# Two PSUM banks in turn for G and V, two long scans, and a state sum made in PSUM

## The chip, the cores and the metric

The kernel runs on one core of one Trainium2 chip. The metric is the device time of one execution in microseconds (us); lower is better. Each engine (PE is TensorE, DVE is VectorE, ACT is ScalarE, POOL is GpSimd) works through its own instruction list in order, and the lists are tied by semaphores alone.

## The reference: what is computed

One sequence of 2048 tokens of width 128 goes through two residual layers. The first is a damped-oscillator state space layer with 4 heads, head width 64 and state size 128; the second is a dense mixture of 8 experts plus a shared one.

```
# layer 1, on layernorm(x); for each head, p = 64 channels, n = 128 states
v = (v - dt*A*y + dt*u*Bv) / denom          # denom = 1 + dt*kdamp + dt^2*A, per head, token and n
y = y + dt*v + dt*u*By
o = sum_n y*Cy + sum_n v*Cv                 # By, Bv and Cy, Cv are l2-normalised over 256
out = (o + skip*u) * silu(z) @ W_out.T
# layer 2, on layernorm(x): softmax router, top 2 of 8 experts (gelu MLPs), plus the shared expert
```

## The kernel before, in words

**Tiling.** Tokens are cut into 16 tiles of 128, and four tiles make a group, so there are four groups g. A (tile, head) pair is a q; a group has 16 of them. The recurrence inside a tile is written with products of 2x2 transition matrices, which are formed for the 16 q of a group at once, forwards and backwards from the middle of a tile (`MID` = 64).

**Stages.** Before group 0 there is a prologue, which prepares the coefficients of that group. Each group then has three stages. The *step loop* runs 32 matrix steps on DVE (L1008), between which DVE also adds the experts of the group before (L1230). The *mid stage* is a software pipeline over k = 0 to 23 (`MID_STEPS`): at k below 16 it handles q = 16g + k, and `due(g, k, lag)` says which tile's work with a given lag falls on k; it puts tile c at k = 3 + 4c + lag. The coefficients of the next group (the "front", `front_early`) are made at fixed k inside it. The *expert stage* follows: second layernorm, router and expert matmuls on PE, gelu on ACT, with the next group's matrices and step loop on DVE at the same time.

**One q in the mid stage.** PE projects B and C into one of two PSUM banks (`proj`, L513) as soon as DVE's `products` of two q earlier have freed it. ACT squares the bank (`pair`, L767). DVE scales half of it in place (`pair`, L1105) and multiplies it with the transition products (`products`, L1122 and L1124). POOL adds these to W and V (`wv`, L1376 and L1379). PE then makes G = V'W in bank GG (L536) and transposes V into bank VT (L540), both in `gv`. DVE masks G (`causal_g`, L1112) and ACT copies V' out (`vt_copy`, L773). `gv(q)` waits for the mask of q-1 and, for its transposes, for the copy of q-1, since there is one bank GG and one bank VT.

**The order on each engine** is the order in which the code calls these, per k: PE: `op`, `proj(k+1)`, `norms_back`, `norms_C`, `tail`, `norms`, `tail_T`, `gv(k-1)`, front. ACT: `pair(k)`, small copies, front, then `vt_copy(k-1)`, with the copy of the norm sums behind each fourth one. DVE: `state_sum`, `pair(k)`, `residual`, `tile_out`, `causal_g(k-2)`, `products(k)`, `state`, `add_skip`, front. POOL: `ubar`, `gates`, `crossings`, `wv(k)`.

**A tile's state.** `tail` makes the tile's contribution in bank RR with ub (64 columns of a head) stationary and the V' of two halves, 256 columns, moving (L572). ACT copies RR to `rts` (L802), `tail_T` transposes it back in four pieces into RR (L598), and DVE's `state_sum` adds it to the state `xi` into `zz` (L1132). `state` applies the tile's transition to `zz` (L1142 to L1146). The output part of `tail` goes to bank OO (L587, L589) and needs `xi`.

**The coefficients.** The log denominators of a group lie in `lden` in 16 segments of 129. DVE makes the running sum of each with one scan (L969, sixteen in all, over k = 15 and 16), one subtraction of the middle column follows (L977, k = 17), ACT takes two exponentials (L717, L720), and DVE makes beta and alpha from them (L983, L991).

Of the kernel before, what the change touches and what calls it, by code (L numbers as in the profile page):

```python
# [32 lines left out]
ALU = mybir.AluOpType  # L33
# [36 lines left out]
PRODUCTS, NORMS, NORMS_C, TAIL, TAIL_T, OUT = 1, 2, 4, 4, 6, 7  # L70
MASK, UBAR, GATES, TILE_OUT, STATE_SUM, STATE = 2, 3, 5, 6, 7, 3
# [25 lines left out]
def build(nc, x, w_inT, dw_wT, dw_bT, w_outT, skipT_in, dt_bias, theta_rawT, k_rawT,  # L97
          router_w, router_b, sw1, sb1T, sw2, sb2, rw1, rb1T, rw2, rb2, out):
    ctx = ExitStack()
    with ctx:  # L100
# [26 lines left out]
        ones = sb("ones", 128, 1)  # L127
        eps_l2 = sb("eps_l2", 128, 1)
# [8 lines left out]
        lraw = sb("lraw", 128, KP)  # L137
        lx = sb("lx", 128, KP)
        le = sb("le", 128, KP)
        lp = [sb(f"lp{i}", 128, KP) for i in range(2)]  # L140
        dtts = [sb(f"dtt{i}", 128, KP) for i in range(2)]
        dtr = sb("dtr", KP, TS)
        lden = sb("lden", NS, PC)
        de = sb("de", NS, 2 * PC)
        ab = sb("ab", NS, 2 * PC)
        DTN, LCS = 1, PC
# [8 lines left out]
        tf = [sb(f"tf{i}", 128, GT * NE * NE) for i in range(2)]  # L155

# [18 lines left out]
        rts = sb("rts", 128, 2, 2, NS)  # L175
# [24 lines left out]
        w9T = sb("w9T", NX, GC)  # L200
# [3 lines left out]
        def bank(name):  # L204
# [3 lines left out]
        GG = bank("GG")  # L208
        VT = bank("VT")
# [21 lines left out]
        scan_done, inv_den, beta_done = sem("scan_done"), sem("inv_den"), sem("beta_done")  # L231
# [4 lines left out]
        gv_done, gm_done, vt_done, norm_done, row_done, ub_done, gate_done = (sem(s) for s in  # L236
            ("gv_done", "gm_done", "vt_done", "norm_done", "row_done", "ub_done", "gate_done"))
        r_done, tail_done, rts_done, rt_done, z_done, y1_done, y3_done, op_done, x2_done, xi_done = (sem(s) for s in
            ("r_done", "tail_done", "rts_done", "rt_done", "z_done", "y1_done", "y3_done", "op_done", "x2_done",
# [43 lines left out]

        block = ctx.enter_context(nc.Block())
# [30 lines left out]
        for g in range(NG):  # L315
            for k in range(MID_STEPS):
                for tile in due(g, k, NORMS):
                    plan("norms", tile)
                for tile in due(g, k, NORMS_C):
                    plan("normsC", tile)  # L320
                if g + 1 < NG:
# [65 lines left out]
        def _(pe):  # L387
# [18 lines left out]
            def front_early(g, k):  # L406
# [16 lines left out]
                if 0 <= k - F_BCAST < NH:  # L423
# [4 lines left out]
                    for c in range(GT):  # L428
                        row = NH * c + h
                        last = pe.matmul(hb[:, c * TS:(c + 1) * TS], ident[0:KP, row:row + 1].broadcast_to([KP, 128]),  # L430
                                         dtr[:], start=True, stop=True)
# [84 lines left out]
            def norms(tile):  # L516

                q = NH * tile
                pe.wait_ge(vt_done, q + NH - 1)
                if tile:  # L520
                    pe.wait_ge(row_done, tile)
                pe.wait_ge(sq_done, q + NH)
                for i in range(2):
                    for h in range(NH):
                        last = pe.matmul(VT[32 * h:32 * h + 1, 2 * TS:4 * TS], ones[:],  # L525
                                         sq[(q + h) % NSQ][:, 2 * i:2 * i + 2, :], start=(i == 0), stop=(i == 1))
                last.then_inc(norm_done, 1)

            def gv(q):
                v, w = vt[q % 2], wt[q % 8]  # L530
                pe.wait_ge(wv_done, q + 1)

                if q:
                    pe.wait_ge(gm_done, q)
                for i in range(2):
                    pe.matmul(GG[:, 0:TS], v[:, i, :], w[:, i, :], start=(i == 0), stop=(i == 1))  # L536
                if q:
                    pe.wait_ge(vt_done, q)
                for i in range(2):
                    last = pe.transpose(VT[:, TS * i:TS * (1 + i)], v[:, i, :], ident[:])  # L540
                last.then_inc(gv_done, 1)

            def norms_back(tile):

                pe.wait_ge(row_done, tile + 1)
# [14 lines left out]
            def tail(tile):  # L560
# [31 lines left out]

            def tail_T(tile):

                pe.wait_ge(rts_done, tile + 1)
                for i in range(2):
                    for j in range(2):
# [877 lines left out]
```

## Time and profile before

| | us |
|---|---|
| median of 3 runs (lowest to highest) | 612.76 (611.01 to 613.66) |
| the profiled execution's own time | 609.62 |
| its span, first to last instruction | 607.9 |
| busy in the span: DVE / PE / PE weight loads | 499.4 / 437.1 / 341.4 |
| busy in the span: ACT / POOL | 261.8 / 207.0 |
| prologue | 0 to 54.9 |
| step loop of group 0 | 54.9 to 90.7, DVE busy 33.68 |
| mid stage of group 0, to the last residual | 90.7 to 169.0 |
| mid stages of groups 1, 2, 3 begin | 223.7, 358.8, 494.4 |
| expert stage of group 3, the last one | 559.6 to 607.9, PE busy 39.48 |

The three lines on busy time are sums over stages with different limits, so they don't say what bounds a stage. PE's records overlap where its instructions are pipelined; the pitch of a series of matmuls is read from the start of the series to the start of the next one. "x8" counts instructions: a matmul of 32-bit numbers is two of them, a transpose is one.

### The profile page before, as it was taken

What the parts mean: (1) busy time and instruction counts of PE and PEld (TensorE: products, weight loads), DVE (VectorE), ACT (ScalarE), POOL (GpSimd) and SP (SyncE); (2) the same over time, 40 slices, a digit from 0 to 9 for tenths busy, and PEclk for the clock granted to TensorE, in tenths of its full rate; (3) what the DMA queues carried; (4) which work ended last, traced back from release to release, by engine and by line L of the source; (5) the groups of instructions that cost most, each with busy time, mean ns of one, the idle gap of its engine ahead of it and who ended that gap; (6) DMA issues with size and microseconds to landing.
All of it is one profiled execution on the core that took longest, in us unless ns stands there. A gap on an engine that the chain in (4) does not pass through costs nothing.

```text
span 607.9 us, 9167 instructions
## 1 busy us (share of the span) xinstructions
PE 437.1 (72%) x3140; PEld 341.4 (56%) x3140; DVE 499.4 (82%) x1270; ACT 261.8 (43%) x435; POOL 207.0 (34%) x268
## 2 busy tenths in 40 slices
PE   2932007996889927896789927896889937985897
PEld 1822006784666726684656726684756636763575
DVE  5389997789989996989999997889999977774332
ACT  1641232454565623354665523453665523332532
POOL 2021006575420016575420026565610036664000
PEclk9967558999899959999999959999989959999799
DMA  7300000000000010000000000000000000000000
GB/s 241 98 0 1 0 1 0 2 2 2 1 1 1 2 35 1 1 1 2 2 1 1 1 19 0 1 2 2 1 0 2 1 17 3 0 2 2 0 1 17
DMA packets 8416, 7.03 MB, mean 12 GB/s; under 512 B 1578, under 2 KB 7603, under 8 KB 8243
## 3 DMA queue, kind: packets, MB, share of 16 engines
q1 hardware_dynamic: 8370, 6.46, 3.6%
q8 instruction: 25, 0.41, 0.3%
q14 instruction: 21, 0.16, 0.1%
HBM read 5.41 MB, written 1.05 MB: 11 GB/s over the span
## 4 chain that ended last, share of the span: by engine, by line
PE 35%; DVE 33%; issue 8%; POOL 7%; ACT 6%; POOLq 0%; DVEq 0%; ACTq 0%
PE HB L480 7%; DVE tp L1008 4%; PE GG L536 4%; PE OO L494 4%; PE BC L513 3%; PE RR L494 3%; DVE hist L1008 3%; DVE mm L1087 3%; DVE pr L1087 2%; DVE mm L1124 2%; DVE ab L969 2%; DVE xr L1230 2%; PE VT L525 2%; DVE mm L1122 2%; POOL rinv L1396 2%
## 5 line engine op out<-in xcount | busy, mean ns | idle before, releaser
L1376 POOL TENSOR_TENSOR big<-mm 128x256 f32<-128x256 f32 x64 | 52.2, 816 | 268.4 <-DVE mm L1124 268.3
L513 PE MATMUL BC<-xnT,winT 128*128 128x128 f32 x512 | 76.8, 297 | 78.1 <-DVE mm L1124 77.5
L513 PEld LDWEIGHTS BC<-xnT,winT 128*128 128x128 f32 x512 | 68.0, 207 | 83.5 <-DVE mm L1124 82.3
L773 ACT ACTIVATE big<-VT 128x256 f32<-128x256 f32 x64 | 24.5, 382 | 157.7 <-PE VT L540 157.7
L480 PE MATMUL HB<-xnT,w 128*128 128x512 f32 x144 | 71.9, 625 | 3.7 <-ACT sqs L832 1.9
L536 PE MATMUL GG<-big,vt 128*128 128x128 f32 x256 | 45.7, 303 | 26.8 <-DVE gtm L1112 23.3
L1105 DVE TENSOR_TENSOR BC<-BC,de 128x256 f32<-128x256 f32 x64 | 27.4, 428 | 37.4 <-ACT hist L767 18.7
L536 PEld LDWEIGHTS GG<-big,vt 128*128 128x128 f32 x256 | 35.2, 199 | 40.6 <-issue 31.1
L751 ACT ACTIVATE pr<-hist 128x512 f32<-128x512 f32 x32 | 34.0, 1115 | 52.9 <-DVE hist L1008 52.9
L1008 DVE TENSOR_TENSOR tp<-big,hist 128x256 f32<-128x256 f32 x124 | 52.1, 420 | 1.4
L1379 POOL TENSOR_TENSOR vt<-mm 128x256 f32<-128x256 f32 x64 | 52.3, 817 | 0.0
L1122 DVE TENSOR_TENSOR mm<-BC,pr 128x512 f32<-128x512 f32 x64 | 43.9, 686 | 1.0 <-issue 0.3
L1124 DVE TENSOR_TENSOR mm<-BC,pr 128x512 f32<-128x512 f32 x64 | 43.6, 681 | 0.0
L480 PEld LDWEIGHTS HB<-xnT,w 128*128 128x128 f32 x144 | 25.1, 198 | 27.9 <-issue 12.7
L494 PEld LDWEIGHTS RR<-w,gtm 128*128 128x128 f32 x288 | 35.1, 192 | 9.6 <-issue 7.3
L494 PEld LDWEIGHTS OO<-w,sqs 128*128 128x128 f32 x288 | 35.2, 192 | 9.4 <-issue 7.2
L1008 DVE TENSOR_TENSOR hist<-tp 128x128 f32<-128x128 f32 x128 | 36.7, 287 | 1.8
L494 PE MATMUL RR<-w,gtm 128*128 128x128 f32 x288 | 36.8, 278 | 0.8 <-ACT sqs L832 0.8
L494 PE MATMUL OO<-w,sqs 128*128 128x128 f32 x288 | 36.7, 277 | 0.8 <-ACT gtm L832 0.8
L1396 POOL TENSOR_TENSOR rinv<-nsq,mhalf 128x8 f32<-128x8 f32 x16 | 28.0, 1750 | 16.7 <-ACT nsq L789 16.7
L445 PE MATMUL HB<-xnT,taps 128*128 128x256 f32 x128 | 33.3, 418 | 0.0
L832 ACT ACTIVATE sqs<-HB,b 128x512 f32<-128x512 f32 x36 | 24.4, 686 | 20.7 <-PE HB L480 20.7
(172 smaller groups left out, 1007.9 us busy)
## 6 DMA issues: line engine op xcount, KB each, us to landing
xr<-in_x SPq DMA_DIRECT2D x4, 256.0 KB, 4.5
winT<-in_w_inT SPq DMA_DIRECT2D x1, 1024.0 KB, 5.9
w<-in_rw SPq DMA_DIRECT2D x1, 1024.0 KB
out<-xr SPq DMA_DIRECT2D x4, 256.0 KB, 2.3
taps<-in_dw_wT SPq DMA_DIRECT2D x1, 512.0 KB, 3.6
w<-in_sw SPq DMA_DIRECT2D x2, 128.0 KB
winT<-in_w_inT SPq DMA_DIRECT2D x1, 130.0 KB, 2.6
winT<-in_w_inT SPq DMA_DIRECT2D x1, 128.0 KB, 3.2
```

The source lines that it names most:

```text
L445: last = pe.matmul(hb[:, j * 2 * TS:(j + 1) * 2 * TS], taps[:, k, j * 128:(j + 1) * 128], xt[:, o + k:o + k + 2 * TS], start=(k == 0), sto ...
L480: pe.matmul(hb[:], w1[:, e, i * 128:(i + 1) * 128], xnT2[:], start=True, stop=True)\
L494: last = pe.matmul(yb[:, c * TS:(c + 1) * TS], h[:, i, c * TS:(c + 1) * TS], w2[:, e, i, :], start=(i == 0), stop=(i == 1 and e != NE))
L513: last = pe.matmul(b[:, j * TS:(j + 1) * TS], winT[:, col:col + NS], xt, start=True, stop=True)
L536: pe.matmul(GG[:, 0:TS], v[:, i, :], w[:, i, :], start=(i == 0), stop=(i == 1))
L751: last = act.activation(view(pr, slot, (SL, 4 * KP), (2 if f else -2, CHUNK)), view(hist, n * CHUNK % RING * ST + f * 4 * KP, (1, 4 * KP), ...
L1008: dve.tensor_tensor(*args).then_inc(step, 1)
L1122: dve.tensor_tensor(m[:, 0:2], view(y, TS, (TS, 2), (0, 2), (1, TS)), view(pr, o + 1, (-1, 2), (SL, 2), (1, TS)), ALU.mult)
L1124: dve.tensor_tensor(m[:, 2:4], view(y, 0, (3 * TS, 2), (0, 2), (1, TS)), view(pr, W0 + o + 1, (0, 2), (SL, 2), (1, TS)), ALU.mult).then_in ...
L1376: pool.tensor_tensor(wt[q % 8][:], m[:, 0], m[:, 3], ALU.add)
L1379: pool.tensor_tensor(vt[q % 2][:], view(m, 5 * TS, (-3 * TS, 2), (1, TS)), view(m, 3 * TS, (TS, 2), (1, TS)), ALU.subtract).then_inc(wv_do ...
L1396: pool.tensor_tensor(rinv[:].rearrange("p i h -> p (i h)"), nsq[:].rearrange("p i h -> p (i h)"), mhalf[:], ALU.pow).then_inc(inv_done, 1)
```

## The change

- **Two banks in turn.** GG and VT become GV0 and GV1. A q's G and its V' both go to bank q % 2, and `gv(q)` waits for the mask and the copy of q-2. The mask now also waits for the copy of the same q. `vt_copy` moves to k = q + 2 on ACT, right behind `pair`, and on DVE `causal_g` moves behind `products`.
- **Norm sums in an HB bank.** They had the right half of VT. They now take a turn in the HB banks (`sums`, at lag 0 instead of 1) and are copied by `sums_copy`.
- **The state.** `tail` first adds `xi` to RR by an identity matmul of 512 columns (not for tile 0), then adds the tile's contribution with V' stationary (128 columns) and 64 columns of ub moving, eight matmuls. RR then holds the sum in the layout that `state` wants, and ACT copies it to `zz`. `tail_T`, the copy to `rts` and `state_sum` go; the last tile makes no RR at all. All of `tail` now waits for `xi`.
- **The scans.** `lden` holds each segment as two halves of 64, all first halves and then all second halves. One scan of 1024 elements runs backwards over the first halves with subtraction and one forwards over the second halves with addition; a multiplier `keep`, 0 at each segment's first element and 1 elsewhere, restarts the sum. The sums come out centred, so the subtraction of the middle goes.
- Small buffers share memory (`lraw`, `lx`, `le`, `lp`, `dtr` lie in the router's scratch, `w9T` in `x1`).

```diff
-PRODUCTS, NORMS, NORMS_C, TAIL, TAIL_T, OUT = 1, 2, 4, 4, 6, 7
-MASK, UBAR, GATES, TILE_OUT, STATE_SUM, STATE = 2, 3, 5, 6, 7, 3
+PRODUCTS, COPIES, SUMS, NORMS, NORMS_C, TAIL, OUT = 1, 2, 0, 2, 4, 4, 7
+MASK, UBAR, GATES, TILE_OUT, STATE = 2, 3, 5, 6, 3
...
-        GG = bank("GG")
-        VT = bank("VT")
+        GV = [bank("GV0"), bank("GV1")]
+        G_COLS, V_COLS = slice(0, TS), slice(TS, 3 * TS)
...
-            def norms(tile):
+            def sums(tile):
 
                 q = NH * tile
-                pe.wait_ge(vt_done, q + NH - 1)
-                if tile:
-                    pe.wait_ge(row_done, tile)
+                hb = h_bank("sums", tile)
                 pe.wait_ge(sq_done, q + NH)
...
             def gv(q):
-                v, w = vt[q % 2], wt[q % 8]
+                v, w, b = vt[q % 2], wt[q % 8], GV[q % 2]
                 pe.wait_ge(wv_done, q + 1)
 
-                if q:
-                    pe.wait_ge(gm_done, q)
+                if q >= 2:
+                    pe.wait_ge(gm_done, q - 1)
+                    pe.wait_ge(vt_done, q - 1)
                 for i in range(2):
-                    pe.matmul(GG[:, 0:TS], v[:, i, :], w[:, i, :], start=(i == 0), stop=(i == 1))
-                if q:
-                    pe.wait_ge(vt_done, q)
+                    pe.matmul(b[:, G_COLS], v[:, i, :], w[:, i, :], start=(i == 0), stop=(i == 1))
                 for i in range(2):
-                    last = pe.transpose(VT[:, TS * i:TS * (1 + i)], v[:, i, :], ident[:])
+                    last = pe.transpose(b[:, TS * (1 + i):TS * (2 + i)], v[:, i, :], ident[:])
...
-                for h in range(NH):
-                    last = pe.matmul(RR[rows(h), (h // 2) * 2 * NS:(h // 2 + 1) * 2 * NS], u[:, head(h)],
-                                     vts[(NH * tile + h) % 8], start=True, stop=True)
-                last.then_inc(r_done, 1)
+                pe.wait_ge(xi_done, tile + 1)
+                if tile < NT - 1:
+
+                    if tile:
+                        pe.matmul(RR[:], ident[:], xi[tile % 2][:].rearrange("p i d -> p (i d)"), start=True, stop=False)
+                    for h in range(NH):
+                        for i in range(2):
+                            last = pe.matmul(RR[:, i * DI + h * HD:i * DI + (h + 1) * HD],
+                                             vts[(NH * tile + h) % 8][:, i, :], u[:, head(h)],
+                                             start=(tile == 0),
+                                             stop=(tile == 0 or (h == NH - 1 and i == 1)))
+                    last.then_inc(r_done, 1)
                 pe.wait_ge(gm_done, NH * (tile + 1))
-                pe.wait_ge(xi_done, tile + 1)
...
-                    for tile in due(g, k, PRODUCTS):
-                        norms(tile)
-                    for tile in due(g, k, TAIL_T):
-                        tail_T(tile)
                     if 0 <= k - PRODUCTS < KP:
                         gv(KP * g + k - PRODUCTS)
+                    for tile in due(g, k, SUMS):
+                        sums(tile)
...
-            def rts_copy(tile):
+            def state_copy(tile):
                 act.wait_ge(r_done, tile + 1)
                 if tile:
-                    act.wait_ge(rt_done, tile)
-                act.activation(rts[:], RR[:].rearrange("p (j i n) -> p j i n", j=2, i=2), ACT.Copy)\
-                    .then_inc(rts_done, 1)
+                    act.wait_ge(x_done, tile)
+                act.activation(zz[:], RR[:].rearrange("p (i d) -> p i d", i=2), ACT.Copy).then_inc(z_done, 1)
...
                     if k < KP:
                         pair(KP * g + k)
+                    if 0 <= k - COPIES < KP:
+                        vt_copy(KP * g + k - COPIES)
...
-                    n = KP // (F_CENTRE - F_SCAN)
-                    for j in range((k - F_SCAN) * n, (k - F_SCAN + 1) * n):
-                        last = dve.tensor_tensor_scan(ab[:, LCS + j * SL:LCS + (j + 1) * SL],
-                                                      ones[:].broadcast_to([128, SL]), lden[:, j * SL:(j + 1) * SL],
-                                                      0.0, ALU.mult, ALU.add)
...
-                    dve.tensor_tensor(view(lden, 0, (SL, KP), (1, SL)), view(ab, LCS, (SL, KP), (1, SL)),
-                                      view(ab, LCS + MID, (SL, KP), (0, SL)), ALU.subtract).then_inc(lcum, 1)
+                    f = k - F_SCAN
+                    run = view(lden, KP * MID if f else KP * MID - 1, (1 if f else -1, KP * MID))
+                    dve.tensor_tensor_scan(run, keep[:], run, 0.0, ALU.mult, ALU.add if f else ALU.subtract)\
+                        .then_inc(lcum, 1)
...
                 dve.wait_ge(gv_done, q + 1)
+                dve.wait_ge(vt_done, q + 1)
...
-                    for tile in due(g, k, STATE_SUM):
-                        if tile % GT < GT - 1:
-                            state_sum(tile)
                     if k < KP:
                         pair(KP * g + k)
...
+                    if k < KP:
+                        products(KP * g + k)
                     if 0 <= k - MASK < KP:
                         causal_g(KP * g + k - MASK)
-                    if k < KP:
-                        products(KP * g + k)
```

## Rows read from the trace of the kernel before

**Rows 1.** Busy time by stage: window, length, busy of each engine (instructions), PE clock, DMA.
```profile
90.68:147.44 56.76, 47.76 (x432) 39.85 (x432) 47.49 (x108) 25.41 (x54) 36.86 (x51) 0.96 0.01 1
147.44:168.96 21.52, 16.28 (x124) 13.23 (x125) 19.94 (x35) 10.57 (x15) 10.69 (x10) 0.92 0.00 1
223.66:283.24 59.58, 47.85 (x432) 39.87 (x432) 50.60 (x112) 25.29 (x54) 37.95 (x52) 0.96 0.00 1
494.37:546.88 52.51, 43.78 (x386) 35.40 (x386) 37.89 (x80) 15.04 (x38) 34.98 (x51) 0.93 0.01 1
```
**Rows 2.** Waits from 90.68 to 147.44: total us, times, longest us.
```profile
DVE BC L1105 <- ACT hist L767: 5.7, 6, 1.2
DVE BC L1105 <- ACT sqs L767: 2.4, 2, 1.7
```
**Rows 3.** Timeline, DVE, PE and ACT together: start, length, instruction [idle before, releaser].
```profile
106.66 0.43 DVE L1105 TENSOR_TENSOR BC<-BC,de 128x256 f32<-128x256 f32 x1 [1.65 <-ACT sqs L767]
107.00 0.28 DVE L1112 TENSOR_TENSOR gtm<-GG,causal 128x128 f32<-128x128 f32 x1
107.80 0.68 DVE L1124 TENSOR_TENSOR mm<-BC,pr 128x512 f32<-128x512 f32 x1
107.43 0.68 PE L536 MATMUL GG<-big,vt 128*128 128x128 f32 x4 [0.80 <-DVE gtm L1112]
107.95 0.38 PE L540 MATMUL VT<-ident,vt 128*128 128x128 f32 x2
108.37 0.38 ACT L773 ACTIVATE big<-VT 128x256 f32<-128x256 f32 x1 [1.74 <-PE VT L540]
108.65 0.59 ACT L767 ACTIVATE sqs<-BC 128x512 f32<-128x512 f32 x1
109.27 0.43 DVE L1105 TENSOR_TENSOR BC<-BC,de 128x256 f32<-128x256 f32 x1 [0.79 <-ACT sqs L767]
```
**Rows 4.** Timeline of PE: series of matmuls and the series behind them.
```profile
108.17 0.95 PE L414 MATMUL HB<-winT,xnT 128*128 128x4 f32 x8
108.98 1.14 PE L513 MATMUL BC<-xnT,winT 128*128 128x128 f32 x8
112.73 1.03 PE L572 MATMUL RR<-big,ub 128*64 128x256 f32 x8
113.59 0.39 PE L587 MATMUL OO<-gtm,ub 128*64 128x128 f32 x4
115.00 0.71 PE L536 MATMUL GG<-big,vt 128*128 128x128 f32 x4
```
**Rows 5.** The chain that ended last: start, length, PE.
```profile
116.82 0.97 PE VT L525 x16
195.71 1.72 PE HB L480 x4
```
**Rows 6.** Timeline of DVE: the scans and the centring, in the prologue and in group 0.
```profile
27.37 5.18 DVE L969 TENSOR_TENSOR_SCAN ab<-ones,lden 128x129 f32<-128x129 f32 x16 [2.54 <-ACT lden L710]
32.59 2.31 DVE L977 TENSOR_TENSOR lden<-ab 128x2064 f32<-128x2064 f32 x1
147.44 4.11 DVE L969 TENSOR_TENSOR_SCAN ab<-ones,lden 128x129 f32<-128x129 f32 x8
151.65 2.64 DVE L969 TENSOR_TENSOR_SCAN ab<-ones,lden 128x129 f32<-128x129 f32 x8
```
**Rows 7.** Groups of instructions over the whole run: busy us, mean ns.
```profile
L1132 DVE TENSOR_TENSOR zz<-xi,RR 128x512 f32<-128x512 f32 x15 | 10.1, 676 | 1.0 <-PE RR L598 1.0
```
**Rows 8.** Timeline of DVE and PE in group 0: scaling of q9 and q14, tile 3's tail, last residual.
```profile
119.88 0.43 DVE L1105 TENSOR_TENSOR BC<-BC,de 128x256 f32<-128x256 f32 x1 [1.13 <-ACT hist L767]
140.33 0.42 DVE L1105 TENSOR_TENSOR BC<-BC,de 128x256 f32<-128x256 f32 x1
158.20 1.08 PE L572 MATMUL RR<-big,ub 128*64 128x256 f32 x8 [0.83 <-POOL ub L1402]
168.96 0.29 DVE L1170 TENSOR_TENSOR xr<-OO,xr 128x128 f32<-128x128 f32 x1 [1.48 <-PE OO L605]
```

More of the change, by code:

```diff
@@ L127, in build @@
         ones = sb("ones", 128, 1)
+        keep = sb("keep", NS, KP * MID)
         eps_l2 = sb("eps_l2", 128, 1)
@@ L136, in build @@
         rstd = sb("rstd", 128, GT)
[L137 to L140, printed above, removed]
         dtts = [sb(f"dtt{i}", 128, KP) for i in range(2)]
-        dtr = sb("dtr", KP, TS)
-        lden = sb("lden", NS, PC)
+        lden = sb("lden", NS, 2 * KP * MID)
         de = sb("de", NS, 2 * PC)
         ab = sb("ab", NS, 2 * PC)
-        DTN, LCS = 1, PC
+        DTN = 1
         szT = sb("szT", 128, 2, GC)
@@ L155, in build @@
         tf = [sb(f"tf{i}", 128, GT * NE * NE) for i in range(2)]
+        dtr = tf[1][0:KP, 0:TS]
+        lraw, lx, le, lp0, lp1 = (tf[0][:, i * KP:(i + 1) * KP] for i in range(5))
+        lp = [lp0, lp1]
         sqs = sb("sqs", NS, 2 * 4 * TS)
@@ L320, in build @@
                     plan("normsC", tile)
+                for tile in due(g, k, SUMS):
+                    plan("sums", tile)
                 if g + 1 < NG:
@@ L591, in tail @@
                 last.then_inc(tail_done, 1)
[L593 to L597, printed above, removed]
-                        last = pe.transpose(RR[:, i * DI + j * 128:i * DI + (j + 1) * 128], rts[:, j, i, :], ident[:])
-                last.then_inc(rt_done, 1)
             def op(tile):
@@ L636, in _ @@
                         tail(tile)
[L637 to L640 removed]
                     if 0 <= k - PRODUCTS < KP:
                         gv(KP * g + k - PRODUCTS)
+                    for tile in due(g, k, SUMS):
+                        sums(tile)
                     if g + 1 < NG:
@@ L763, in pair @@
                 if q >= NSQ:
-                    act.wait_ge(norm_done, (q - NSQ) // NH + 1)
+                    act.wait_ge(h_ready, h_read_of("sums", (q - NSQ) // NH))
                 if q % KP == 0:
@@ L857, in _ @@
                         norms_C_copy(tile)
+                    for tile in due(g, k - 1, SUMS):
+                        sums_copy(tile)
                     for tile in due(g, k - 1, TAIL):
-                        rts_copy(tile)
+                        if tile < NT - 1:
+                            state_copy(tile)
                     if g + 1 < NG:
@@ L1252, in _ @@
             dve.memset(xnTs[0][:, 0:HALO], 0.0)
-            dve.memset(VT[:], 1.0)
             identity_states()
-            dve.memset(view(lden, 0, (SL, KP), (1, 1)), 0.0).then_inc(cst, 1)
+            dve.memset(view(de, MID, (SL, 2 * KP), (1, 1)), 1.0)
+            dve.memset(keep[:], 1.0).then_inc(cst, 1)
             dve.wait_ge(cst, 1)
+            dve.memset(view(keep, 0, (MID, KP), (1, 1)), 0.0).then_inc(cst, 1)
+            dve.wait_ge(cst, 2)
             front_early(0, F_STATS)
@@ L1317, in _ @@
                 if g + 1 < NG:
-                    state_sum(GT * (g + 1) - 1)
                     matrices(g + 1, 0)
```

98 lines of the change are left out of this document (42 added, 56 removed).

## The prediction

> **What bounds the kernel now.** I read the busy time by stage first, then who waits for whom in the mid stage, then the timeline of the engines side by side, and the pitches of PE's series last. By stage, no engine is full in the mid stage of group 0: of 56.76 us DVE is busy 47.49 and PE 47.76, in group 3, which prepares no further group, 37.89 and 43.78 of 52.51 [rows 1]. Two engines at 84% that alternate in idling point to a loop through several engines, not to a full one. The waits name the place: DVE's scaling of a projection (L1105) waits 5.7 + 2.4 = 8.1 us for ACT's square in the mid stage of group 0 [rows 2]. The timeline shows why [rows 3]. DVE masks G of one q at 107.00; PE, which has waited for that, makes the next G at 107.43 and the transposes at 107.95; ACT copies the transpose at 108.37 and only behind it squares the next projection at 108.65, though that projection had long been ready; DVE scales at 109.27, and then masks again. The ring is 109.27 - 106.66 = 2.61 us, while DVE's own four instructions take about 1.75 (0.34 to the mask, 0.80 for the mask and the first half of `products`, 0.6 for the second half), and PE's two series about 1.85 (the projection 1.14 less the overlap, so 1.09 [rows 4], then 0.52 + 0.22 [rows 3]).
>
> In the last third of a mid stage (147.44 to 168.96) DVE is busy 19.94 of 21.52 us [rows 1]: the scans, the centring, beta and alpha bind there, with the last tiles' states. Step loops and the expert stages aren't touched.
>
> **The change part by part.** All sums are made in the profiled execution (609.62 us, span 607.9); the median of the runs is 612.76, 0.5% above it, and I carry the difference in us over to it.
>
> *The ring.* Two banks and the copy one k later cut both edges: `gv(q)` needs the mask of q-2, and the square no longer stands behind the copy of q-1. What remains is DVE at 1.75, PE at 1.85, and the loop products, projection, square, scaling, products over two q: 1.09 + 0.6 + 0.34 + 1.2 and some 0.3 of handing over, so 3.5 for two q. Up to 0.75 us per q goes where only the ring binds. That is k = 2 to 6 and the plain k between tiles.
>
> *PE's added work.* Removed per tile: RR by 64 stationary columns, 113.59 - 112.73 = 0.86 us [rows 4], and four transposes at the 0.11 of those in [rows 3] (0.22 for two), 0.44; in all 1.30. Added: an identity matmul of 512 columns, two instructions at 1.72/4 = 0.43 [rows 5], 0.86; and 16 instructions with 128 stationary and 64 moving columns, a shape that the trace does not have. With 4 moving columns eight take 108.98 - 108.17 = 0.81, 0.101 each; with 128 the eight of the projection take 0.136 each [rows 4]. That bounds it from 1.6 to 2.2 us. I take 0.12 and so 1.9, in the middle, since the weight loads set the pitch at few columns and 64 lies between. Net 1.5 us per tile (0.6 for the first, -1.3 for the last, which makes no RR), 20 us of PE work in the run; bounds 15 to 25.
>
> The Trainium skill speaks against this very form: TensorEngine Tiling (Array Packing), section Performance Considerations, says that where the moving side has at most 64 columns one should swap it with the stationary side and use column tiling, which is what the kernel does now and gives up. The trace agrees as far as it goes (0.86 us for the old form against at least 1.6 for the new); the sum above already carries it, and the rule's remedy would keep 0.7 to 1.3 us per tile.
>
> *What order adds.* RR now waits for `xi`, so 2.8 us and then the 1.4 us of OO (115.00 - 113.59 [rows 4]) stand in series behind DVE's `state`, and behind them on PE stand `gv`, the sums and the next projection. Before, RR lay ahead of that wait. The norm sums (0.97 us, [rows 5]) do as much as before and take a turn in the HB banks: at k = 11 the broadcast for the front must wait until ACT has read the norm transposes of the same k, but the sums themselves cover those 0.9 us. If the cover were gone it would cost some 0.5 us in each of three groups. ACT's copy to `zz` is as long as the one to `rts` and nothing more waits behind it. The mask's second wait is for a copy that precedes it by a whole `products` (1.3 us); the memsets of `keep` lie before the first DMA lands. I cost these at nothing.
>
> *What DVE loses.* `state_sum`: 0.60 to the next start, 0.676 alone, 15 times [rows 7]. The scans: 16 took 5.18 us in the prologue, 0.324 each, and 4.11 + 2.64 in group 0, where POOL works beside them [rows 6]. How much of 0.324 is per element the rows don't say. If all, 2.5 ns, two scans of 1024 take 5.1 us; if as other DVE instructions here 0.07 is fixed, 2.0 ns, and they take 4.2. With POOL beside them at the 0.514 of the slower eight it could be 8.2; at the 1.04 ns of a multiplication it would be 2.3. I take 4.4 in the prologue and 5.4 in the groups. The centring of 2.31 [rows 6] goes wholly. In the prologue all of this is one chain from Ln to the exponential: 5.18 + 2.31 - 4.4 = **3.1 us** gained (bounds -0.7 and 5.2).
>
> For the scans a page has the rate: the Trainium skill, DVE: opcode table, instruction layouts, handler registers and perf-mode slots, section Datapath and trigger behaviour, says that the built-in scan runs at half throughput. At half of the 1.04 ns per element this trace shows, two scans would take an estimated 4.4 us; by a reading of the row as all per element they take 5.1, and 0.7 us of the prologue's gain would be lost.
>
> *The group's sum.* I carry group 0's timeline forward from its own starts, each instruction at its earliest under the new waits. k = 2, 3 are held by POOL's `crossings` and rstd (xn starts at 98.66 either way). Then DVE ends `products(6)` at 107.8, before at 111.1: 3.0 us ahead. Tile 0's tail on PE gives 0.6 back and the log polynomial (3.1 us on DVE) hides part; q9 is scaled at 117.8, before at 119.88 [rows 8]. At k = 11 PE has the longer tail, the sums and a broadcast, 8.5 us in all, and DVE is 0.7 us *behind* at the third `lden` product (134.5, before 133.8): the gain is gone there. With `state_sum` off DVE it is 0.9 ahead at k = 14 (139.4, before at 140.33 [rows 8]). The long mask-and-scan knot at 147 to 152 (PE idle behind a mask that is behind eight scans) dissolves; `xi` of tile 3 comes at 156.6, before at 160.3. Then PE: 2.8 + 1.4 (tail), 4.6 (u and z), 0.55 (op), so the last residual is at 166.0, before at 168.96 [rows 8]: 3.0, and with the last `state_sum` **3.6 us** for group 0. Groups 1 and 2 have a `state` of 2.1 us at k = 6 as well (59.58 us against 56.76 [rows 1]); it now falls where PE is late anyway, which gives 1 us more: **4.6 us** each. In group 3 the same steps end with a tail of OO alone behind `xi`, where PE waited for ub before [rows 8]: **2.2 us**. With the prologue 3.1 + 3.6 + 4.6 + 4.6 + 2.2 = 18.1. Handing over is never as tight as in such a replay, and denser work makes DVE and POOL slow each other more often; I take off a tenth: **16.5 us**. Profiled execution 593.1, median 596.3.
>
> **The rivals.**
>
> *PE eats the gain.* The new bound in the middle of a mid stage is PE. If its pitch is 0.136, or the clock (0.96 over group 0's middle [rows 1]) drops more often, the 16 tails cost 25 us, of which all but the ring's slack shows: the groups give 1 to 2 us each and the prologue 3, so 606. For it: k = 11 is already lost in my sum at 0.12. Against it: a third of a mid stage is DVE's, where PE's extra work lies beside.
>
> *Slower.* The one mechanism is the serial tail: z, `state`, RR, copy, `state`, with `gv` and `proj` behind RR on PE in order. If each tail pushes PE's next projection by the whole 2.8 us, as RR now stands behind `xi` (bound in 15 tiles), that is +42, less 8 per mid stage from the ring and 13 from scans and `state_sum`: about 617. It decides as soon as `xi` comes later than PE reaches the tail in most tiles; in group 0 before that is so only in tiles 2 and 3 (RR at 158.20 waits for ub even so [rows 8]).
>
> *More than I say.* At 0.101 per instruction, with the scans at 4.2 us also in the groups and all of the 8.1 us of waits [rows 2] gone, the groups give 5 to 7 each: 587.
>
> *The change doesn't do what it says.* The two long scans, in place and one of them backwards, run at the contended rate of 4 ns per element, 8.2 us a group: prologue 0.7 us later, groups 2.5 us less each: 607.
>
> **How the numbers follow.** Forecast 0.60 (590 to 602 around it), more than that 0.13, PE eats the gain 0.15, slow scans 0.05, slower by the serial tail 0.07. 0.5% (3 us) is about what a measurement of this kernel tells from no change. Of the middle rivals a third ends within 3 us of before: faster 0.86, same 0.07, slower 0.07. The range is 586 to 608: it takes in the other cases but for the slower one and the outer edge of the best.
>
> **What would show it.** Right: the scaling L1105 no longer waits for ACT's square at k = 3 to 6, and q follow at 1.8 to 2.1 us there; masks stand behind `products`; PE near 0.9 busy from the first tail on; two scans of 2.2 to 2.7 us per group and alpha's end some 3 us earlier; PE's RR series of about 1.9 us behind an identity of 0.86. Wrong: PE's series at 0.136 or above, DVE waiting at L1105 for squares because the projection is late in most k, a scan above 3 us, or PE's clock below 0.9 in the mid stages.

## The result and the profile after

The changed kernel takes **618.43 us** (median of 5 runs, 616.72 to 618.77), the kernel before 612.76 beside it: ratio 1.0092, 95% interval 1.0061 to 1.0123. The forecast was 596.3, faster. The interval leaves out 1, so the change made it slower, by 0.9%. Two executions of the experiments below are left out of the ratios: one of "identity last" took 738 us at a granted clock of 0.63, and one of experiment 7 took 618.06. The profiled execution has a span of 616.9 us (before 607.9), DVE busy 485.4 (499.4), PE 463.2 (437.1).

What was forecast of the single pieces came nearly to the tenth. In DVE's timeline the ring turns in 1.93 us, against 2.61 in [rows 3], and at k = 3 to 6 no square is waited for (over the whole run L1105 waited 37.2 us for ACT's squares, its counterpart L1092 waits 8.7):

```profile
99.53 0.42 DVE L1092 TENSOR_TENSOR BC<-BC,de 128x256 f32<-128x256 f32 x1
101.26 0.28 DVE L1100 TENSOR_TENSOR gtm<-GV,causal 128x128 f32<-128x128 f32 x1
101.46 0.42 DVE L1092 TENSOR_TENSOR BC<-BC,de 128x256 f32<-128x256 f32 x1
```

Two long scans take 4.47 us in the prologue, 2.84 and 2.28 in group 0, against 5.18 and 6.75 and a centring of 2.3 in [rows 6]:

```profile
27.51 4.47 DVE L964 TENSOR_TENSOR_SCAN lden<-keep,lden 128x1024 f32<-128x1024 f32 x2 [2.53 <-ACT lden L708]
143.63 2.84 DVE L964 TENSOR_TENSOR_SCAN lden<-keep,lden 128x1024 f32<-128x1024 f32 x1
151.82 0.29 DVE L1100 TENSOR_TENSOR gtm<-GV,causal 128x128 f32<-128x128 f32 x1 [5.35 <-PE GV L542]
152.03 2.28 DVE L964 TENSOR_TENSOR_SCAN lden<-keep,lden 128x1024 f32<-128x1024 f32 x1
168.71 0.29 DVE L1150 TENSOR_TENSOR xr<-OO,xr 128x128 f32<-128x128 f32 x1 [2.22 <-PE OO L606]
```

The third of these rows is the loss. Between the scans DVE sits 5.35 us behind a G of PE. The timeline of PE says what PE did then. First a tail as it should be (tile 1, from 123.17), then the tail of tile 2 (from 141.93):

```profile
123.17 1.10 PE L577 MATMUL RR<-xi,ident 128*128 128x512 f32 x2 [0.31 <-DVE xi L1126]
124.10 1.89 PE L580 MATMUL RR<-ub,big 128*128 128x64 f32 x16
125.93 0.44 PE L596 MATMUL OO<-gtm,ub 128*64 128x128 f32 x4
...
141.93 2.05 PE L577 MATMUL RR<-xi,ident 128*128 128x512 f32 x2 [3.22 <-DVE xi L1126]
143.76 3.52 PE L580 MATMUL RR<-ub,big 128*128 128x64 f32 x16
147.21 0.70 PE L596 MATMUL OO<-gtm,ub 128*64 128x128 f32 x4
147.69 1.07 PE L598 MATMUL OO<-big,xi 128*64 128x128 f32 x8
149.97 1.12 PE L540 MATMUL GV<-big,vt 128*128 128x128 f32 x4
```

PE waits 3.22 us for `xi`, and the same instructions then take 8.04 us (141.93 to 149.97): 1.83 for the identity against 0.93, 3.45 for the sixteen instructions behind it against 1.83. The granted clock of this stretch is 0.50, and 1.00 over tile 1's tail: it is the lower of TensorE's two levels, 1.2 GHz against 2.4. In group 3 the wait is 3.20 us too, but the level falls later: the identity still takes 0.93 us there and the sixteen behind it 2.96. `gv`, which DVE waits for, stands behind all of it. The granted clock by stage is 0.87 from 145 us on and 0.92 ahead of it, where [rows 1] have 0.92 and 0.96.

```profile
87.75:145.00 57.25, 49.37 (x418) 41.71 (x418) 49.89 (x106) 27.02 (x54) 37.57 (x53) 0.92 0.01 1
145.00:168.00 23.00, 20.02 (x155) 16.95 (x155) 14.62 (x18) 9.91 (x14) 12.41 (x9) 0.87 0.00 1
```

The waits of the whole run (engine, line, releaser: total, times, longest) show the three that grew (before: 13.5 us at the gate, 1.5 for the mask behind PE, none ahead of RR):

```profile
POOL gate L1390 <- ACT rcb L792: 45.3, 15, 6.0
DVE gtm L1100 <- PE GV L542: 27.4, 6, 7.0
PE RR L577 <- DVE xi L1126: 19.0, 11, 3.2
```

Laid over each other from the first scaling of a group (us from there, read off the DVE timelines), with the experiments below. "Last mask" is the mask of q15, "next group" the first scaling of group 1:

| group 0 | q9 | q15 scaled | last mask | last residual | next group |
|---|---|---|---|---|---|
| before | 29.20 | 55.04 | 63.84 | 78.28 | 132.98 |
| changed | 26.99 | 53.95 | 67.51 | 80.96 | 135.46 |
| fillers | 26.95 | 53.91 | 63.17 | 76.62 | 131.13 |
| identity last | 26.96 | 53.63 | 62.00 | 74.16 | 128.97 |
| V-stationary, sum on DVE | 26.98 | 53.16 | 61.54 | 73.58 | 128.29 |
| banks and scans, state as before | 26.38 | 51.90 | 60.29 | 72.33 | 127.05 |
| banks alone | 26.41 | 51.94 | 61.05 | 74.81 | 129.52 |
| scans alone | 29.20 | 55.03 | 63.34 | 77.64 | 132.55 |

In groups 0 to 2 of the changed kernel q15's scaling comes sooner than before, and what is lost is lost behind it: in group 0 13.56 us to the last mask against 8.80. The stages lose 2.5, 1.4 and 1.0 us in groups 0, 1 and 2. Group 3, from its first scaling to the end, loses 7.1: there q15's scaling is already 1.5 us later than before (52.21 against 50.70), and the last mask 7.1 us. The prologue gains 2.9.

### The profile page after: what moved, and what is told of

Read it like the earlier page. It is cut to its first block, busy times and chain, and to the rows that moved or that the text cites. A ratio compares the mean times of both kernels' runs of the same rounds, so it can differ in the third digit from the quotient of the medians.

```text
span 616.9 us, 9232 instructions
## 1 busy us (share of the span) xinstructions
PE 463.2 (75%) x3216; PEld 367.8 (60%) x3216; DVE 485.4 (79%) x1193; ACT 268.5 (44%) x434; POOL 212.4 (34%) x268
## 4 chain that ended last, share of the span: by engine, by line
PE 32%; DVE 23%; issue 6%; POOL 6%; ACT 3%; POOLq 0%; DVEq 0%; ACTq 0%
PE HB L485 6%; PE RR L580 4%; DVE tp L995 3%; PE OO L499 3%; DVE xr L1210 3%; PE RR L499 3%; PE HB L450 2%; PE RR L577 2%; DVE mm L1112 2%; DVE mm L1074 2%; PE OO L598 2%; DVE hist L995 2%; DVE pr L1074 2%; PE GV L540 2%; PE BC L518 1%
## 5 line engine op out<-in xcount | busy, mean ns | idle before, releaser
L1354 POOL TENSOR_TENSOR big<-mm 128x256 f32<-128x256 f32 x64 | 50.1, 782 | 257.0 <-DVE mm L1112 256.9
L518 PE MATMUL BC<-xnT,winT 128*128 128x128 f32 x512 | 75.5, 294 | 76.4 <-DVE mm L1112 76.2
L771 ACT ACTIVATE big<-GV 128x256 f32<-128x256 f32 x64 | 24.6, 384 | 103.1 <-PE GV L542 102.1
L1357 POOL TENSOR_TENSOR vt<-mm 128x256 f32<-128x256 f32 x64 | 58.9, 920 | 0.0
L540 PE MATMUL GV<-big,vt 128*128 128x128 f32 x256 | 45.5, 304 | 6.1 <-POOL vt L1357 6.1
L540 PEld LDWEIGHTS GV<-big,vt 128*128 128x128 f32 x256 | 36.6, 206 | 13.4 <-POOL vt L1357 8.5
L580 PEld LDWEIGHTS RR<-ub,big 128*128 128x128 f32 x240 | 35.3, 226 | 8.5 <-issue 8.5
L1100 DVE TENSOR_TENSOR gtm<-GV,causal 128x128 f32<-128x128 f32 x64 | 18.1, 282 | 27.7 <-PE GV L542 27.4
L1390 POOL TENSOR_TENSOR gate<-rcb,szT 128x256 f32<-128x256 f32 x16 | 22.3, 1392 | 45.3 <-ACT rcb L792 45.3
L765 ACT ACTIVATE hist<-BC 128x512 f32<-128x512 f32 x38 | 22.4, 596 | 33.0 <-PE BC L518 32.8
```

What stands on the lines that cost most here:

```text
L518: last = pe.matmul(b[:, j * TS:(j + 1) * TS], winT[:, col:col + NS], xt, start=True, stop=True)
L540: pe.matmul(b[:, G_COLS], v[:, i, :], w[:, i, :], start=(i == 0), stop=(i == 1))
L580: last = pe.matmul(RR[:, i * DI + h * HD:i * DI + (h + 1) * HD], vts[(NH * tile + h) % 8][:, i, :], u[:, head(h)], start=(tile == 0), stop ...
L1354: pool.tensor_tensor(wt[q % 8][:], m[:, 0], m[:, 3], ALU.add)
L1357: pool.tensor_tensor(vt[q % 2][:], view(m, 5 * TS, (-3 * TS, 2), (1, TS)), view(m, 3 * TS, (TS, 2), (1, TS)), ALU.subtract).then_inc(wv_do ...
```

## Experiments

My theory after the result: the banks and scans gain, and the new state path takes more, by a wait for `xi` that now stands ahead of RR and by TensorE's lower level behind it. The rivals: the banks' new order costs; or the clock is a side effect and PE's added work is the loss.

**1 to 3. The parts apart.** The changed kernel with the old RR form, `tail_T` and `state_sum` back (the edit in short):

```diff
-    pe.wait_ge(xi_done, tile + 1)               # ahead of RR
-    pe.matmul(RR[:], ident[:], xi ...); 8 x matmul(RR, vts stationary, u moving)
+    4 x matmul(RR, u stationary, vts moving); pe.wait_ge(xi_done, tile + 1)   # then OO
+    rts_copy (ACT), tail_T (PE), state_sum (DVE) as before
```

> The changed kernel with the old state path put back (V' as 256 moving columns, copy to rts, four transposes, state_sum); banks in turn and long scans stay. Theory 1 (the loss is all in the new tail: RR in series behind xi, and TensorE at its lower clock after the wait for xi): the gains that the changed kernel has until q15 of each group and in the prologue come through, 598 to 604 us. Rival 2 (the banks' new order costs: POOL's gate now waits 45.3 us for ACT's copy of the norms, the mask waits 27.4 us for gv, and DVE and POOL slow each other): still 612 us or above.

Measured 585.34 us, ratio 0.9568 (0.9536 to 0.9601); once more later, 585.75, 0.9591 (0.9553 to 0.963). The rival on the banks is out, and my own range for it was too timid: without the new state path the change gains 25 us. The new state path costs 33 (32 by the ratios, each against the kernel before of its own series).

The kernel before with the long scans alone:

> The kernel before with nothing but the two long scans per group (and the small buffers that share memory to make room). Both theories: the prologue is 2.9 us shorter, as in the changed kernel. Theory 1: the groups gain 1.5 to 2.5 us each too, because DVE is the bound in the last third of a mid stage when PE isn't late; 602 to 607 us. Rival 3 (in the groups the scans hide behind PE's tail anyway): 609 to 610 us, the prologue alone.

608.58, ratio 0.9963 (0.9944 to 0.9982): less than the prologue's 3.0 us. Of the groups only the first gains, 0.4 us; the others lose 0.7 to 1.2. The timeline of group 0 shows where the shorter scans go. DVE is through with them sooner, but PE then waits 3.16 us for POOL, its projection behind that takes 1.92 us instead of 1.06, the transposes of the state are late, and DVE waits for them:

```profile
149.94 0.71 PE L540 MATMUL GG<-big,vt 128*128 128x128 f32 x4 [3.16 <-POOL vt L1373]
150.74 1.92 PE L517 MATMUL BC<-xnT,winT 128*128 128x128 f32 x8
152.88 1.06 PE L602 MATMUL RR<-ident,rts 128*128 128x128 f32 x4
153.98 0.69 DVE L1123 TENSOR_TENSOR zz<-xi,RR 128x512 f32<-128x512 f32 x1 [2.36 <-PE RR L602]
```

The kernel before with the new state path alone:

> The kernel before with nothing but the new state path (identity matmul and V' stationary into RR, ACT copy to zz, no state_sum; RR waits for xi); banks, order and scans as before. Theory 1: slower than before by the whole of what the changed kernel loses, 622 to 632 us, with PE waiting 2 to 3 us for xi at tile 2 of a group and RR and OO of that tile taking 7 to 8 us where 4.2 is the sum at the higher clock. Rival 2: within 3 us of before, 610 to 616 us.

631.69, ratio 1.0333 (1.0279 to 1.0387). The time is as expected: on either ground the new state path costs 3 to 5%. The way there isn't. At tile 2 of group 0 PE waits for `xi` 1.58 us, and RR and OO behind it take 4.22 (147.67 to 151.89) at a granted clock of 1.00; among the tails that make RR the lower level comes only at tile 3 of groups 1 and 2, behind waits of 2.75 us. The mean granted clock of the profiled execution is 0.90, as in those of the kernel before beside it. So most of the 21 us lost here isn't the clock.

**4. The clock alone.** At the third tile of each group ten identity matmuls of 128 columns fill the wait for `xi`:

```diff
+    if tile % GT == 2:
+        for _ in range(10):
+            pe.matmul(RR[:, 0:TS], ident[:], ident[:], start=True, stop=True)
     pe.wait_ge(xi_done, tile + 1)
```

> The changed kernel with ten identity matmuls of 128 columns (2.7 us) into RR ahead of the wait for xi, in the third tile of each group alone; their result is overwritten. Theory 1, clock part: PE isn't idle there, TensorE stays at its higher clock, the tail of that tile takes 4.2 us in place of 8.0, so up to 3.8 us less per group: 604 to 609 us. Rival 4 (the clock is a side effect, the wait itself is the loss): 618 us or, by the matmuls' own time where xi is early, up to 620.

602.83, ratio 0.9861 (0.9834 to 0.9888): 15.6 us less (14 by the ratios) with forty matmuls more that compute nothing. The wait for `xi` ends at the same time as without them, but the tail behind it takes 4.25 us (141.67 to 145.92) and not 8.04:

```profile
138.85 2.50 PE L575 MATMUL RR<-ident 128*128 128x128 f32 x20 [0.31 <-POOL ub L1383]
141.67 1.12 PE L580 MATMUL RR<-xi,ident 128*128 128x512 f32 x2 [0.32 <-DVE xi L1129]
142.63 1.89 PE L583 MATMUL RR<-ub,big 128*128 128x64 f32 x16
145.92 0.71 PE L540 MATMUL GV<-big,vt 128*128 128x128 f32 x4
```

The Trainium skill, TensorE: Matmul & The Clock Gate, section Part 1: The HAM clock gate, says that the slow level is the resting state and that activity releases the full one. The trace agrees: the granted clock from 138.85 to 145.92 is 1.00 with the fillers.

**5, 6. The order.** The contributions (eight matmuls, sixteen instructions; the expectations count these) ahead of the wait, the identity matmul last:

```diff
-    pe.wait_ge(xi_done, tile + 1)
-    if tile: pe.matmul(RR[:], ident[:], xi ..., start=True, stop=False)
     8 x pe.matmul(RR[...], vts ..., u ...)
+    pe.wait_ge(xi_done, tile + 1)
+    if tile: pe.matmul(RR[:], ident[:], xi ..., start=False, stop=True)
```

> Alone changed against the changed kernel: in the tail, the sixteen V-stationary contributions stand ahead of the wait for xi and the identity matmul of xi stands last, still accumulating. Same matmuls, same count. Theory 1 (the state path costs because RR stands in series behind xi, and the wait ahead of it lets TensorE fall to its lower clock): at the tile whose xi comes 3.2 us late, 1.9 us of the wait is now filled with matmuls and 1.9 us of work leaves the way from xi to OO, so y, the last residual and the ring come earlier than in the run with filler matmuls, which kept the clock but not the order. 594 to 601 us, and PE's wait for xi 1.3 us or less. Rival (only the clock costs; the order is indifferent): the same time as with fillers, 602 to 605. Rival (the added PE work itself costs, 1.5 us a tile): not below 602.

594.42, ratio 0.9721 (0.9699 to 0.9743). The rows below are from the same kernel once more:

> The same kernel as the one with the identity matmul last, for one more profile. Theory 1: PE waits for xi 1.3 us at the third tile of a group and its OO behind it takes about 1.4 us, as at the higher level of TensorE's clock; last mask of group 0 at 8.5 to 9.5 us behind q15's scaling, and the last residual about 12.5 us behind that. Rival: the clock still falls there, and OO takes 2.8 us.

592.98. The granted clock stays at 1.00 and OO takes 1.46 us (142.42 to 143.88), as my theory had it; the wait is 0.81 us, shorter than its 1.3, and the last mask comes 8.37 us behind q15's scaling:

```profile
138.55 2.00 PE L577 MATMUL RR<-ub,big 128*128 128x64 f32 x16 [0.31 <-POOL ub L1382]
141.37 1.12 PE L584 MATMUL RR<-xi,ident 128*128 128x512 f32 x2 [0.81 <-DVE xi L1128]
142.42 0.44 PE L598 MATMUL OO<-gtm,ub 128*64 128x128 f32 x4
143.88 0.71 PE L540 MATMUL GV<-big,vt 128*128 128x128 f32 x4
```

It beats the fillers by 8 us without any idle work. Order costs by itself, beside the clock.

**7, 8. `gv(k-1)` ahead of the tail**, in the changed kernel and in the version of 585 us:

```diff
-    for tile in due(g, k, TAIL): tail(tile)
     if 0 <= k - PRODUCTS < KP: gv(KP * g + k - PRODUCTS)
+    for tile in due(g, k, TAIL): tail(tile)
```

> Alone changed against the changed kernel: in PE's step, G and V of the pair before stand ahead of the tail, so the mask and the copy of V don't wait behind PE's wait for xi. Theory 1: the wait for xi stays (about 3 us, less the 1.1 us of matmuls now ahead of it) and so does most of the lower clock behind it, but the mask's wait on GV (27 us in six places) goes: 607 to 613 us. Rival (what the queue behind PE's wait costs is the whole loss): 600 to 604. Rival (GV itself waits for POOL's vt there, so nothing moves, or the tail comes later): 616 to 622.

> The version with the two-bank form and the long scans but the state path of before (585.3 us), with G and V of the pair before ahead of the tail. In its trace PE idles 2.2 us ahead of OO at the tile before the last of a group while GV of the pair before stands behind it. Theory 1: the 1.1 us of GV moves into this idle time, 1 us a group at most: 580 to 584. Rival (in most steps the tail isn't waiting, and GV's wait for POOL's vt, up to 1.8 us, now delays the tail): 586 to 592.

607.41, ratio 0.9928 (0.9899 to 0.9957), and 591.77, 0.9686 (0.9665 to 0.9708). The mask's wait goes in the first, the slow level stays. In the second, where there was no such wait, 6 us are lost, and 5.7 of the 6.5 us of span between the two profiles lie in group 3, 4.4 of them ahead of q14's scaling. In group 0 the loss is 0.7 us; its rows show PE waiting for POOL ahead of the tail and at the lower level behind it (the eight instructions of RR in 1.70 us, otherwise 0.87). That group 3 loses by the same mechanism is not shown but for its last tail, where RR takes 1.77 us:

```profile
139.02 1.22 PE L542 MATMUL GV<-big,vt 128*128 128x128 f32 x4 [2.29 <-POOL vt L1374]
140.60 1.87 PE L576 MATMUL RR<-big,ub 128*64 128x256 f32 x8
142.30 0.39 PE L591 MATMUL OO<-gtm,ub 128*64 128x128 f32 x4
```

**9. Banks alone**, on the kernel before, short scans and centring kept:

> The kernel before with the two-bank form of G alone (G and V of a pair in one of two banks, sums of squares in an HB bank, mask behind the products, copy of V first in ACT's step), and the short scans, centring and old state path of before. Theory A (the parts add: banks and long scans together gave 25 us and the scans alone 2): 586 to 591 us. Theory B (the parts need each other: with sixteen short scans and the centring in DVE's steps 14 to 16 the two banks are used up behind them, as the queue before DVE was): 593 to 600 us, with q15's mask and y later than in the run of both.

598.38, ratio 0.9779 (0.974 to 0.9818). Banks 12.7 us, scans 2, both 25: about 10 us are had only by the two together. In the table the banks alone are level with both up to q15 and lose 2.5 us behind it, where the centring stands. In the profiles groups 1 and 2 are 2.8 and 3.9 us longer than with both, and group 3, which has no scans, 1.6.

**10. PE's work by itself.** Twelve identity matmuls ahead of RR in every tail of the 585 us version:

> The version with the two-bank form, the long scans and the state path of before (585.3 us), with twelve identity matmuls of 128 columns put ahead of RR in every tail: 12 by 0.12 is 1.5 us a tile of added TensorE work, as much as the V-stationary form adds net; RR's own matmuls overwrite what they leave, so nothing of the result changes. The question is what part of the 9 us that the V-stationary form still loses once its order is mended (594.4 against 585.3) is the added work. Theory 1 (it is the work, of which more than a third lies on the way at three or four tiles of a group): 590 to 597 us. Rival (PE has room in the tail, the added work is hidden, and the 9 us come from the copy of the state through ACT and its later z): 585 to 588 us.

607.84, ratio 0.9956 (0.9938 to 0.9974), 22.5 us more. The expectation had an error of mine in it: a matmul is two instructions here, so the twelve are 24 and take 2.87 us a tile (141.55 to 144.42), 46 us in the run, not 24:

```profile
141.55 2.94 PE L576 MATMUL RR<-ident 128*128 128x128 f32 x24 [0.32 <-POOL ub L1399]
144.42 1.08 PE L578 MATMUL RR<-big,ub 128*64 128x256 f32 x8
```

So half of what is added to PE in the tail shows in the time. Net the new state path adds 1.5 us a tile (sixteen instructions 1.83 to 1.93 and the identity 0.93, less 0.87 and 0.44 of the old), 22 us in the run. Half of that is 11, an estimate; what is left of the loss once the order is mended is 9 (594.4 less 585.3), so the added work can account for all of it.

**11, 12. ACT's order.** The copy of V behind the copies of the norms, in "identity last" and in the 585 us version:

> The kernel with the contributions ahead of the wait for xi and the identity matmul last (594.4 us), and in ACT's step the copy of V behind the copies of the norms in place of ahead of them, as before the change. Theory 1: the copy of V waits for GV, which stands behind PE's tail, and the copies of the norms wait behind it; with that off, POOL's wait for them at the gate (45 us in the changed kernel) falls below 20 and 1 to 3 us of it are on the way: 591 to 594. Rival (the copy of V is what the mask waits for, so it comes later and the ring with it): 596 to 602.

> The version with the two-bank form, the long scans and the state path of before (585.3 us), with the copy of V behind the copies of the norms in ACT's step. There POOL waits for the norms at the gate only 10.5 us in all. Theory 1: nothing is to be had, and the mask, which waits for the copy of V now, comes a little later: 585 to 590. Rival: ACT's order was costly here too: 580 to 584.

594.86, ratio 0.9728 (0.97 to 0.9756), and 585.83, 0.9592 (0.9557 to 0.9627): no change in either, though POOL's wait at the gate fell from 23.4 to 7.0 us in the first. That wait, the one that grew most in the changed kernel, is beside the path in these two versions.

**13 to 17. Which form the 9 us belong to.** V-stationary contributions, but no identity matmul and no copy by ACT; DVE adds `xi` and RR:

> Two-bank form and long scans as in the change, and of the new state path the V-stationary contributions alone: sixteen matmuls at 0.12 us into RR (1.9 us) ahead of the wait for xi; no identity matmul and no copy of the state by ACT; DVE adds xi and RR into zz at its old place, 0.68 us. Against the state path of before (585.3 us) PE has 1.9 us in place of 8 by 0.136 and four transposes (1.1 and 0.6), and ACT's copy and the transposes' wait are gone; against the changed kernel with the identity matmul last (594.4 us) PE has 0.86 us a tile less, while xi isn't waited for twice. Theory 1 (added TensorE work in the tail lands on the end almost whole, as twelve added matmuls did with 1.4 us a tile of 1.5; the 9 us of the mended order are the identity matmul): 0.86 to 1.0 us by 15 tiles is 13 to 15 us less than 594.4, and 0.8 us a tile ahead of OO, less 0.6 behind it, more than the state path of before: 580 to 588 us. Rival (the V-stationary form itself costs, by sixteen short matmuls ahead of OO in place of eight): 591 to 597.

> As the run with V-stationary contributions and DVE's sum, with the sum one step of DVE earlier (step 6 in place of 7), which the missing transposes allow. Theory 1: zz isn't what is late, and the sum ahead of y and of the mask delays these by 0.7 us: 0 to 3 us more than its twin. Rival: xi comes earlier by it and the tail's OO with it: 1 to 4 us less than its twin.

> The two-bank form and long scans with the state path of before once more, beside the two above on the same chip: 584 to 587 us, and the difference to the V-stationary form with DVE's sum within 3 us if that form costs nothing by itself.

592.67 (0.9699, 0.9672 to 0.9727), 593.54 (0.9714, 0.969 to 0.9737), 585.75. My theory, built on the 1.4 of 1.5 us of experiment 10, had 580 to 588 and missed. 5.6 of the 8.8 us of span between the first and the last lay in group 3, where the last tile makes a contribution that nobody reads, at the lower level, ahead of OO:

```profile
534.27 3.68 PE L575 MATMUL RR<-ub,big 128*128 128x64 f32 x16 [1.14 <-POOL ub L1378]
537.87 0.70 PE L591 MATMUL OO<-gtm,ub 128*64 128x128 f32 x4
```

So I left it out, there and in the state path of before:

```diff
-    for h in range(NH):
+    for h in range(NH if tile < NT - 1 else 0):
```

> V-stationary contributions with DVE's sum (592.7 us), without the contributions of the last tile, whose state nothing reads. In its trace they stood ahead of that tile's OO for 3.60 us, at half the pace of the other tiles (0.23 us a matmul against 0.12), and OO behind them took 2.8 us against 1.4; of the 7 us to the state path of before 5.6 lay in group 3. Theory 1 (the V-stationary form costs about 1 us in each of groups 0 to 2, and group 3's excess is these sixteen matmuls): 588 to 590 us. Rival (OO starts at the lower level all the same and the wait for the state's addend takes their place, as in the changed kernel, where the last tile had no contributions either and OO came 2 us later than its inputs): 591 to 593.

> The state path of before with the two-bank form and the long scans (585.3 us), without the contribution, ACT's copy and the transposes of the last tile. There eight matmuls took 0.91 us ahead of OO at the higher level. Theory 1 (TensorE's granted clock decides): TensorE then starts OO after an idle time of 2 us instead of behind work, OO takes up to 2.8 us instead of 1.4, and the 0.9 us are given back: 585 to 587. Rival (work left out is time won): 584.0 to 584.8.

590.15 (0.9667, 0.9621 to 0.9714) and 587.08 (0.9595, 0.9534 to 0.9656). The first is at the edge of what theory 1 expected. The second is no faster than its parent; its runs spread from 583.72 to 590.02, and the profiled one took 4.6 us and 6.1 us more between q9 and q13 of group 1 than the two profiles of its parent, at a granted clock of 0.83 where both of these have 0.91 (its row, then that of the parent's second profile):

```profile
214.60:273.00 58.40, 51.96 (x405) 44.19 (x407) 48.10 (x105) 26.75 (x53) 34.09 (x51) 0.83 0.00 1
```

```profile
214.60:273.00 58.40, 50.30 (x437) 42.23 (x437) 54.34 (x112) 27.13 (x54) 38.43 (x54) 0.91 0.01 1
```

**The best version** of the study is the two banks and the long scans with the state path of before, 585.3 to 585.8 us, 4.1 to 4.3% below the kernel before and some 5% below the changed one.

## Why the prediction was wrong, step by step

- **Ring**: right. Pitch about 1.85 forecast, 1.93 measured. The replay had q9 27.1 us and q14 48.7 behind the first scaling; they came at 26.99 and 48.66.
- **Scans and prologue**: right. 4.4 and 5.4 us forecast, 4.47 and 5.12 measured; prologue 3.1 against 2.93.
- **PE's instructions**: right as durations at the higher level. 1.9 us for the sixteen against 1.83 to 1.93, 0.86 for the identity against 0.93.
- **"What order adds": this step failed.** It says that 2.8 and 1.4 us stand in series behind `xi`, with `gv` behind them, and then costs them inside a replay at the higher level. It never asked how long PE stands idle ahead of them. The replay had `xi` of tile 3 done at 65.9 us and the last residual at 75.3; they came at 71.5 and 80.96, and q14's scaling, the last point that it names ahead of them, was on time: the gap opens in the tail of tile 2. There PE waits 3.2 us, in each of the four groups, because RR now waits too; with RR ahead of the wait, 0.9 us of it is filled and 2.22 are left. The fillers put the lower level at 14 to 16 us of the run, identity-last puts the series behind `xi` at 8 more. The granted clock of 0.87 behind 145 us is one of the prediction's own signs of being wrong.
- **Group 3** misses by most: 2.2 us gained in the sum, 7.1 lost. Against the version of 585.75 us it is 12 us longer in the profiles, 1.8 by q9's scaling, 4.1 by q14's and 10.7 by the last mask. The fillers give back 3.1 of them and the order 3.5 more. This group prepares no further one, so DVE has less other work beside PE's tails; that this is why is not tested.
- **PE's added work**: its 20 us were put partly beside other work, rightly: of the added matmuls of experiment 10 half show. What remains once the order is mended is 9 us: 3 to 4 for the identity with ACT's copy (594.4 against 590.15 without them, 3.3 by the ratios) and the rest for the V-stationary form, which is not settled: 6.9 with the last tile's contributions in both (592.67 against 585.75), 3.1 without them in both (590.15 against 587.08, whose runs spread over 6 us).
- **The swap given up** cost what the prediction's paragraph on it allowed: the old form takes 0.87 us ahead of OO, the new one 1.83 to 1.93. The Trainium skill, TensorEngine Tiling (Array Packing), section Performance Considerations, speaks against the new form, and the two forms side by side agree (592.67 against 585.75 us).
- **Mis-sized the other way**: the other two parts together are worth 25 us, more than the 18 of the whole sum. I did not foresee that 10 us come only by scans and banks together.
- **Rivals**: "slower, the serial tail" (617, chance 0.07) named the mechanism and nearly the time, but that the time fits is luck: its own terms, 42 less 8 per mid stage and less 13, give 610 us with the four mid stages that there are, and 617 only with three. Its condition was wrong too. It asked that `xi` be late in most tiles; one tile in four that is 3.2 us late is enough when the wait also halves TensorE's clock for the next 8 us. That I had put the clock under another rival and the serial tail under this one is why neither got its due.

## What to carry to other kernels

When a matmul series moves behind a wait, cost three things: the series, what stands behind it in PE's queue, and the same series at half the clock if PE now has nothing to do during the wait (the next section shows that the length of the wait alone doesn't decide that). Keep what does not depend on the late operand ahead of the wait, and let the dependent matmul accumulate last. Price a change of several parts by part: here 25 us of gain and 33 us of loss came in one change.

## What the runs showed of the hardware

- The idle time ahead of a series does not tell by itself whether TensorE will be slow. The same OO behind the same 2.22 us took 1.46 us in one execution of the 585 us version, at a granted clock of 1.00, and 2.76 in the other (139.71 to 142.47), at 0.50:

```profile
139.71 0.69 PE L591 MATMUL OO<-gtm,ub 128*64 128x128 f32 x4 [2.22 <-issue]
140.16 1.09 PE L593 MATMUL OO<-big,xi 128*64 128x128 f32 x8
142.47 0.99 PE L542 MATMUL GV<-big,vt 128*128 128x128 f32 x4
```

  There a long scan of DVE hid the 1.3 us: the spans are 583.7 and 582.1, and the slower OO belongs to the shorter one.
- Behind a wait of 1.3 us (V-stationary with DVE's sum, 139.7 to 141.0) the level also fell, for some 3.5 us, and so it did in the kernel before behind 1.08 us (tile 3's OO, 2.69 us at a granted clock of 0.52). Behind 0.81 us (identity last), 1.31 (tile 3 of the changed kernel) and 1.58 (experiment 3, tile 2) it did not.
- DVE's product y L1144 took 902 ns on average, before 623, and as much in every version with two banks. Single ones take 0.42, 0.97 or 1.52 us; the long ones lie beside POOL instructions for nearly their whole length, but so do some of the short ones. No run separates that.
